# First norm's factors ahead of the second four scatters, its statistics in rounds 8 and 12; expert results scaled in place on VectorE and copied by ScalarE

## The reference, cut to what matters

```
x = L0_attn_x                                  # 16 x 512 x 256, float32
x = x + attention(layernorm(x))                # 16 heads of 16, a band of at most 60 keys on each side
x = x + moe(layernorm(x))

# moe: 8 experts, 2 of them for each token
gating = softmax(X @ Wg + bg);  top 2 indices of it
h  = silu((X @ W1[e] + b1[e]) * (X @ W3[e] + b3[e]))
y  = h @ W2[e] + b2[e]
out = sum over the two experts of gate * y, then @ Wf + bf
```

## Time and profile before

| what | value |
|---|---|
| median of 3 runs (lowest to highest) | 1390.75 us (1387.23 to 1391.78) |
| the profiled execution's own time | 1396.48 us |
| its span, first to last instruction | 1394.8 us |
| mean granted TensorE clock | 0.947 of 2.4 GHz |
| busy: PE, DVE, ACT, POOL | 86%, 68%, 55%, 43% of the span |
| attention steps | about 118 to 820 us |
| experts | about 828 us to the end |

### The profile page before, as it was taken

The page is one execution under the profiler, slowest core; times in us unless marked ns, Lnnn a source line. Parts: engine busy times, 40 slices in busy tenths (PEclk is TensorE's granted clock), DMA queues, the critical chain, the costliest instruction groups (busy, mean ns, idle before and its releaser), DMA issues. The chain is left out here.

```text
span 1394.8 us, 47057 instructions
## 1 busy us (share of the span) xinstructions
PE 1199.2 (86%) x18189; PEld 883.1 (63%) x18205; DVE 955.1 (68%) x2145; ACT 772.0 (55%) x1344; POOL 605.6 (43%) x651
## 2 busy tenths in 40 slices
PE   4689888889888888888887439999999999999995
PEld 3456555455555455555554228888888888888885
DVE  7245767777777677767775437777677767777775
ACT  1256777777677777767657214444444444444442
POOL 3121142644546445454434633444444445444444
PEclk9889999999999999999998669999999999999998
DMA  5386374665656647564542444566645654644443
GB/s 173 112 212 188 90 199 108 181 171 133 199 148 185 150 131 206 145 188 122 155 134 71 154 138 55 71 127 123 121 55 72 139 104 66 127 66 65 63 67 46
DMA packets 210988, 176.48 MB, mean 127 GB/s; under 512 B 115451, under 2 KB 175483, under 8 KB 210827
## 3 DMA queue, kind: packets, MB, share of 16 engines
q1 hardware_dynamic: 153482, 116.86, 33.5%
q0 software_dynamic: 25728, 34.17, 13.8%
q10 hardware_dynamic: 31616, 23.19, 6.1%
HBM read 66.95 MB, written 89.89 MB: 112 GB/s over the span
## 5 line engine op out<-in xcount | busy, mean ns | idle before, releaser
L1027 DVE TENSOR_REDUCE mx<-p_max 128x4 f32<-128x496 f32 (+1 forms) x248 | 213.1, 859 | 144.0 <-PE p_max L1295 140.8
L1574 PE MATMUL p_h<-xt_parts,w_hi 128*128 128x256 f16 x1824 | 276.0, 274 | 11.2 <-DVE xt_parts L1660 11.1
L837 ACT ACTIVATE probs<-p_exp,unscale 128x736 f32<-128x736 f32 (+1 forms) x256 | 210.4, 822 | 94.4 <-PE p_exp L1295 81.9
L1722 POOL DMA_INDIRECT out<-yw,tokens x136 | 218.2, 1605 | 42.9 <-POOL tick L1721 28.2
L1574 PEld LDWEIGHTS p_h<-xt_parts,w_hi 128*128 128x128 f16 x1824 | 177.7, 98 | 36.9 <-DVE t L1664 11.9
L1664 DVE SCALAR_TENSOR_TENSOR t<-p_h,b,t 128x256 f32<-128x256 f32 x272 | 126.3, 480 | 106.5 <-ACT t L1613 104.9
L1721 POOL TENSOR_TENSOR tick<-tick 128x1 f32<-128x1 f32 x136 | 69.6, 512 | 275.9 <-DVE yw L1687 275.9
L1613 ACT ACTIVATE t<-p_h,b,undo 128x256 f32<-128x256 f32 x272 | 142.2, 558 | 79.4 <-PE p_h L1574 70.6
L1574 PE MATMUL p_h<-xt_parts,w_lo 128*128 128x256 f16 x912 | 175.2, 274 | 0.0
L706 POOL TENSOR_TENSOR qk_lo<-qf,qk_hi 128x512 f16<-128x512 f32 x64 | 76.5, 1200 | 172.5 <-ACT qk_hi L821 172.5
L1618 ACT ACTIVATE hf<-t 128x512 f32<-128x512 f32 x136 | 85.7, 630 | 110.2 <-DVE t L1664 110.2
(11 more groups left out here) (272 smaller groups left out, 2494.3 us busy)
## 6 DMA issues: line engine op xcount, KB each, us to landing
qk_dram<-qk_hi SPq DMA_DIRECT2D x128, 128.0 KB
qs<-qk_dram SPq DMA_DIRECT2D x64, 192.0 KB, 4.2
ks<-qk_dram SPq DMA_DIRECT2D x64, 192.0 KB, 4.4
x_in<-in_x SPq DMA_DIRECT2D x64, 128.0 KB, 2.4
qk_dram<-qk_lo SPq DMA_DIRECT2D x64, 128.0 KB
w_mat<-in_W ACTq DMA_DIRECT2D x32, 256.0 KB
out<-x_sb SPq DMA_DIRECT2D x64, 128.0 KB
w_split<-w_first_hi SPq DMA_DIRECT2D x24, 256.0 KB
```

The costliest lines, as they stand in the source:

```text
L837: nc.scalar.activation(probs[r % 3][:, :, 0:hi - lo].rearrange("p (e s) w -> p e s w", e=2), p_exp[:, :, 0:2 * WIN].rearrange("p e (s w) - ...
L1027: nc.vector.tensor_reduce(out=maxes, in_=max_buffer(r, p_max, p_exp)[:, :, 0:2 * WIN].rearrange("p e (s w) -> p e s w", s=2)[:, :, :, 0:hi ...
L1574: last = nc.tensor.matmul(p_h[:, m % KC, k, :], w[e][a][:, k, HID * c + P * m:HID * c + P * m + P], xt[:, x, c, :], start=(n == 0 and c == ...
L1722: nc.gpsimd.indirect_dma_start(out=io["out"].rearrange("b s d -> (b s) d"), out_offset=bass.IndirectOffsetOnAxis(ap=tokens[:, b, :].bitcas ...
```

## The change

The wait for the attention of batch `i` is taken out of POOL's list, and `norm(i + 4)` stands ahead of `scatter(i - 3, 1)`. DVE takes the two halves of the first norm's `bn_stats` in rounds 8 and 12 and combines them in round 12. In the experts, DVE scales `y` in place directly behind `take_result` and ahead of the second `split`, without waiting for `s_sc`; ACT, behind its token copies and their wait, copies each half from `y` to `yw`. POOL waits for `yw` alone.

```diff
-NORM_ROUND, HIGH_ROUND = 9, 11
+NORM_ROUND, HIGH_ROUND, STATS_ROUNDS = 9, 11, (8, 12)
 ...
                 if stored_expert(i) is not None:
                     low_weights(stored_expert(i), 2)
+                if exists(i + 4):
+                    norm(i + 4)
                 if exists(i - 3) and i - 3 < PROMPT:
                     scatter(i - 3, 1)
-                if exists(i):
-                    pool.wait_ge(s_att, 2 * i + 1)
-                if exists(i + 4):
-                    norm(i + 4)
 ...
                     if exists(i + 4):
-                        if n in (11, 12):
-                            norm_part_stats(i + 4, range(2 * (n - 11), 2 * (n - 11) + 2))
-                        if n == 14:
+                        if n in STATS_ROUNDS:
+                            part = STATS_ROUNDS.index(n)
+                            norm_part_stats(i + 4, range(2 * part, 2 * part + 2))
+                        if n == STATS_ROUNDS[1]:
                             first_stats(i + 4)
 ...
             def load_words(at, g):
-                after(act, s_tok, NB * g)
                 after(act, s_yw, NB * g)
 ...
-            def take_tokens(g):
+            def send(g):
                 act.wait_ge(s_words, 16 * g + 16)
                 for b in range(NB):
+                    act.wait_ge(s_yg, NB * g + b + 1)
                     after(act, s_sc[b], 16 * g)
-                    nc.scalar.activation(tokens[:, b, :], words[:, b, M_TOKEN:M_TOKEN + 2], ACT.Copy).then_inc(s_tok, 1)
+                    nc.scalar.activation(tokens[:, b, :], words[:, b, M_TOKEN:M_TOKEN + 2], ACT.Copy)
+                    nc.scalar.activation(yw[:, b, :], y[:, b, :], ACT.Copy).then_inc(s_yw, 1)
 ...
                 for b in range(NB):
-                    after(dve, s_sc[b], 16 * g)
-                    nc.vector.scalar_tensor_tensor(yw[:, b, :], y[:, b, :], words[:, b, M_GATES + 2 * e:M_GATES + 2 * e + 2].bitcast(F32),
-                                                   kept["bf_half"][:], ALU.mult, ALU.add).then_inc(s_yw, 1)
+                    nc.vector.scalar_tensor_tensor(y[:, b, :], y[:, b, :], words[:, b, M_GATES + 2 * e:M_GATES + 2 * e + 2].bitcast(F32),
+                                                   kept["bf_half"][:], ALU.mult, ALU.add).then_inc(s_yg, 1)
 ...
                 split(e, g, p, 0)
                 if p is not None:
                     take_result(before, p)
+                    weigh(before, p)
                 split(e, g, p, 1)
-                if p is not None:
-                    weigh(before, p)
 ...
                     if p is not None:
                         pool.wait_ge(s_tick, NB * p + b + 1)
-                    pool.wait_ge(s_tok, NB * g + b + 1)
                     pool.wait_ge(s_yw, NB * g + b + 1)
```

More of the change, by code:

```diff
@@ L1508, in build_experts @@
         s_r, s_y, s_yw, s_tick = sem("s_result"), sem("s_y"), sem("s_yw"), sem("s_tick")
-        s_tok = sem("s_tok")
+        s_yg = sem("s_y_weighed")
         s_sc = [sem(f"s_ysc{b}") for b in range(NB)]
@@ L1641, in body @@
                 if p is not None:
-                    take_tokens(p)
+                    send(p)
             at = None
@@ L1652, in _ @@
             load_words(at, last_tile)
-            take_tokens(last_tile)
+            send(last_tile)
         @block.vector
```

## The result

| what | before | after |
|---|---|---|
| median (lowest to highest) | 1388.99 us (1386.29 to 1391.78, 4 runs) | 1372.36 us (1372.04 to 1377.45, 4 runs) |
| ratio | 1 | 0.9871 [0.9842, 0.9901] |
| profiled execution, own time | 1396.48 us | 1372.04 us |
| first to last exponential of the attention | 652.3 us | 637.9 us |
| first `p_h` to last `p_y` of the experts | 557.6 us | 549.0 us |

The change gives 16.6 us. The forecast was 6.7 (1384.1 us, range from 1376), so the sign was right and the size far too small. The profiled execution of before is 7.5 us above its median and that of after is at its own, so the pair of profiles shows 24.4 us, of which some 7 are the choice of the execution.

The account below looks back on a forecast made before the run. PE, busy 86% of the span, was taken to bound the kernel, through its waits and half clock. Terms -9.5 + 3.8 + 0 - 1 = -6.7 us gave 1384.1 us for the median, with an 8-in-10 range of 1376 to 1391.5.

Parts of the forecast that it names:

- The experts: Experts' loop: earlier scaling starts scatters about 0.7 us sooner, ACT gains two copies a tile; -1 us, bounds -2.8 to +3.2.
- Rival B: Experts: the loop through the scatters relaxes, PE's 12.7 us of waits go almost whole; -10 us, 1375; chance 0.08.
- Rival C: Experts: ACT's loop with the copies becomes the pace, from a copy of 0.53 us on; +5.7 us, 1396.5; chance 0.09.
- The norm ahead of the scatters: Attention steps: `shift` comes earlier, so ACT's 10.1 us of waits for it go; -9.5 us, bounds -7.8 and -10.4.
- DVE in rounds 8 and 12: Attention steps: combining the statistics earlier delays DVE's maxima and PE behind them; +3.8 us, bounds 0 and 10.4.
- Rival A: Attention: DVE eats the gain, each of steps 0 to 11 paying 0.87 us, 10.4 in all; 1390.6; chance 0.17.
- `w_all` behind the scatters: Odd attention steps 5, 7, 9, 11: DVE would stand 0.8 us for `w_all`, covered; 0 us, uncovered 3.2.
- Rival D: Attention: scatters hold `w_all` 4.8 us in four steps, delaying DVE; +19 us less 3 of cover, 1400; chance 0.04.

Follow-up runs that it names:

- attention_only: Kernel before with only the attention part of the change (norm ahead of the second four scatters, statistics in rounds 8 and 12), experts as before: ratio 0.9996.
- attention_again: The same kernel as attention_only, run again on other chips against the kernel before: ratio 0.9989.
- order_only: Kernel before with only GpSimd's order changed: norm ahead of the second four scatters, no wait for the attention, statistics as before: ratio 0.9991.
- stats_only: Kernel before with only the first norm's statistics moved to rounds 8 and 12, GpSimd's list as before: ratio 0.9996.
- stats_7_8: Changed kernel with the first norm's statistics in rounds 7 and 8 in place of 8 and 12: ratio 0.9933 to the kernel before.
- attention_third: The same kernel as attention_only, run a third time on other chips against the kernel before: ratio 1.0013.
- spread_before: Kernel before with the eight attention scatters of a step issued in pairs at four places, not in fours at two: 1450.00 us, ratio 0.9884.

## Why the prediction was wrong, step by step

**The experts, forecast -1, measured -9.1 and -9.5 as a part and -8.6 in the stage.** This is the step that failed; it makes up 8.3 of the 9.9 us by which the forecast was short. The first half of the step was right: the first indirect DMA of a tile was to start about 0.7 us sooner, and it starts 2.75 us behind the start of `take_result` in place of 3.57 (medians of the 68 tiles). What was mis-sized is how much of that PE gets. The text gave it 0.3 us in each of eight places, and nothing for the clock. (Eight times 0.3 are 2.4 us; the bound of 2.8 and the -1 that it took follow from no row.) It made the discount because the landings might follow the weight loads. The runs show that they follow the issue: from issue to landing the medians are 3.8 us before and 3.9 after, and ACT stands for a landing in only six places. PE's waits for the columns fell by 5.3 us, and 3.2 of these lie in two tiles alone (2.48 to 0.53 and 2.65 to 1.36 us). The half-clock stretches behind just these two waits went as well, 3.7 us of busy time. The ceiling of 12.7 us held for the waits; the forecast gave away too much of it and set the clock aside.

Rival B named this mechanism, with a chance of 0.08. Its size (-10) came near partly by luck: it had nearly all of the 12.7 us going, and less than half did; the clock made up the rest. The time from the last `p_y` to the end, 1.6 us shorter in after, can't be counted for this part: `attention_only` and `attention_again`, with the experts of before, have 10.6 and 10.7 us there, and the other five such kernels 12.2 to 12.3.

**Rival C** did not come: the copy is 0.40 us, as forecast, and the stage shows no slower pace. Its turning point, a copy of 0.53 us in the order as changed, no run tested. But the order counts for more than the copy. With the scaling late and the same 0.40 us copy the stage is 53 us longer than in after, 0.8 us for each of 68 tiles.

**The norm ahead of the scatters, -9.5.** The mechanism is as forecast: wait 10.1 to none, drain 0.14 us, steps 6 and 8 at 40.9 and 41.2 where "about 41" was said. The size is not shown. It was read from one slow execution; in the other profile of the same attention the wait is 6.5 us, and steps 6 and 8 are as short as in after with the norm where it was. On the chips with standstills the part gave nothing. The prediction set a rule against its row there: the Trainium skill (Perfetto Trace Analysis, DMA Instruction — SWDGE (GPSIMD)) puts the profiled end of such a DMA where the last DSP has written its descriptors. It read this as if nothing of the scatters were left then. The same section says that the data may still be moving at that end, so the rule leaves room for the long drain, and does not speak against it. The 0.14 us, in after and in `order_only`, agree that the drain is the scatters' doing.

**DVE in rounds 8 and 12, +3.8.** The waits came about as forecast: PE's waits for the maxima grew by 5.2 us (3 to 4 were forecast), step 4 by 1.1 us (0.6), rounds 13 and 14 of the even steps by 0.2 to 0.4 and 0.3 us. As time the 3.8 us are not shown: `stats_only` is at 0.9996 and at most 2.5 us slower, and `stats_7_8`, which should have won them back, won nothing. Rival A's 10.4 did not come.

**`w_all` behind the scatters, 0.** DVE's wait is 5.0 us in 4 places (the text had 4 times 0.8, all covered), longest 1.3, and the odd steps are shorter, not longer. Rival D, scatters that hold `w_all` as they held the drain, came in no run: with the statistics late DVE waits 18.0 us, but `w_all` follows the last scatter at once.

**The clock in the odd steps** had no term. Of steps 5, 7 and 9 all are below 1.00 in before, all again in the other profile of the same attention, none in after (its step 3 has such a dip, behind a gap of 1.75 us, and its steps 6 and 8 have one each). Over the whole attention the granted clock is 0.95 in before, 0.97 in that other profile and 0.97 in after, so it is no more than a part of the gain. In before one dip in each of steps 5, 7 and 9 follows a gap of PE of 1.7 to 1.8 us about 9 us into the step, where ACT's exponentials are late, such as this one in step 7:

```profile
416.16 0.45 PE L1288 MATMUL p_exp<-mask,ident_bf 64*64 64x368 bf16 x4 [1.74 <-ACT probs L837]
```

In after the longest gap thereabouts is 1.01 us. That the one causes the other is not shown, and part of the record is against it. The second dip of step 9 in before, at 528.92 us, and those of steps 6 and 8 in after stand behind gaps of no more than 0.94 us. The other profile has the gap of 1.8 us in step 7 with no dip behind it, and a dip later in that step.

**The sum.** 16.6 us less 9.3 of the experts leaves 7.3 for the attention, against the forecast's 5.7. With the intervals (about 4 us on the whole, 3.5 on the part) this can't be told from it. It is a remainder, and that it comes near the forecast may be luck: no run measured the attention part alone on a chip without standstills, which was wanted and not had.

## What to carry to other kernels

When an engine that takes its list in order waits often for a landing, ask which instruction ahead of the DMA could be issued earlier, and follow the few longest waits of the bottleneck engine back to it: here two of 14 waits gave most of what there was to win. An average gain for each place hides that. A wait can also cost what the clock does behind it: look for slow matmuls after the longest ones. And take a second profile before sizing a term from the waits of one, since here the same attention took 639 and 652 us.

## What the runs showed of the hardware that was not expected

- A `drain` of GpSimd shortly behind four indirect DMAs lasted 4.78 us (3.0 to 6.0 in five places of before), and 0.14 us without them.
- On four chips ScalarE or VectorE, or both, stood 1.4 to 5.3 us (`attention_third`) at nearly every group of four indirect DMAs of 128 rows, while TensorE worked with gaps (before: 1467 to 1476 us instead of 1389); in the traces of the result and on one later chip not at all. With the DMAs in pairs the rounds concerned were about 1.2 to 1.7 us longer (even steps of `spread_before`).
- An ACT copy of 128x256 takes 0.40 us, one of 128x512 0.60 us, and one of 2 elements a row 0.20 us.
- PE at half clock behind a gap of 2.65 us: four `p_h` matmuls 1.06 us instead of 0.61. In the attention, half-clock stretches also began behind gaps of 0.94 us, and one gap of 1.8 us had none behind it.
